# A two-layer transformer block on one core: row sends in turns, owner search over partitions, later roots, idle products in the third kernel

## What is computed

```
xn = layernorm(x)
x  = x + attention0(xn) + ffn0(xn)      # 16 causal heads of 16, residual and norm inside; 2 of 8 experts per sequence
xn = layernorm(x)
x  = x + attention1(xn) + moe1(xn)
```

```
for _ in range(6):                      # iterative inverse of kernel 2, per head 64 x 64
    KV = K @ V
    V = 0.25 * V @ (13*I - KV @ (15*I - KV @ (7*I - KV)))
SV = (kernel1 @ V) @ (kernel3 @ v);  out = SV @ w_proj
```

## Time and profile before

| what | us |
|---|---|
| median of three runs | 2002.76 |
| the profiled execution | 2008.18 |
| its span in the trace | 2006.5 |
| TensorE busy | 1745.2 (87%) |
| VectorE busy | 1530.2 (76%) |
| ScalarE busy | 1015.0 (51%) |
| GpSimd busy | 538.1 (27%) |
| granted TensorE clock, mean | 0.951 |

### The profile page before, as it was taken

One profiled execution on the slowest core, in us unless ns is written; L12 is line 12 of the kernel. 1 busy time (PEld: TensorE's weight loads), 2 busy tenths in 40 slices (PEclk: granted clock), 3 DMA queues, 4 the chain that ended last, 5 costly groups with the idle time before them and its releaser, 6 DMA issues. The chain is left out here.

```text
span 2006.5 us, 34424 instructions
## 1 busy us (share of the span) xinstructions
PE 1745.2 (87%) x11935; PEld 926.1 (46%) x12021; DVE 1530.2 (76%) x3643; ACT 1015.0 (51%) x1941; POOL 538.1 (27%) x623
## 2 busy tenths in 40 slices
PE   0898946889999999999999978978677888999998
PEld 0465621223232323232323235645575657888854
DVE  7997649988988989898999938678566994444456
ACT  3464422566767676767676835357413544232210
POOL 0343243000000000000151010045405884666610
PEclk9999976999999999999999988998787999999999
DMA  3466575005040505050551155122215224666566
GB/s 105 152 199 220 186 193 117 1 2 162 2 163 2 162 3 162 3 148 17 153 139 52 43 183 173 64 80 90 95 46 203 97 94 124 192 186 191 166 227 218
DMA packets 162940, 241.33 MB, mean 120 GB/s; under 512 B 21939, under 2 KB 131507, under 8 KB 161107
## 3 DMA queue, kind: packets, MB, share of 16 engines
q1 hardware_dynamic: 126930, 155.08, 25.9%
q0 software_dynamic: 23136, 75.65, 10.7%
q10 hardware_dynamic: 12704, 8.39, 1.4%
HBM read 118.86 MB, written 119.82 MB: 119 GB/s over the span
## 5 line engine op out<-in xcount | busy, mean ns | idle before, releaser
L1118 ACT ACTIVATE c_prob<-c_pst 128x512 f32<-128x512 f32 (+1 forms) x1152 | 578.8, 578 | 301.5 <-PE c_pst L1083 122.9
L1226 DVE TENSOR_REDUCE c_mx<-c_pf 128x2 f32<-128x1024 f32 x384 | 459.4, 1221 | 35.2 <-PE c_pf L1060 31.9
L1079 PE MATMUL c_pst<-c_qa,c_ka 128*128 128x512 bf16 (+3 forms) x1194 | 339.2, 355 | 14.4 <-DMA c_qa<-c_mT 5.8
L1095 PE MATMUL c_po<-c_prob,c_vh 128*32 128x512 f32 (+3 forms) x2560 | 295.7, 544 | 1.0 <-ACT c_prob L1118 0.4
L1060 PE MATMUL c_pf<-c_ka,c_qa 64*128 64x512 bf16 (+3 forms) x1280 | 230.1, 367 | 50.3 <-DMA c_ka<-s_kbias 22.5
L1222 DVE CUSTOM_DVE_ANT_0 c_spare<-c_pf,c_cut 128x384 f32<-128x384 f32 (+3 forms) x512 | 230.8, 491 | 28.6 <-PE c_pf L1060 24.3
L1079 PEld LDWEIGHTS c_pst<-c_qa,c_ka 128*128 128x128 bf16 x1280 | 110.2, 97 | 202.8 <-ACT c_prob L1118 110.1
L1060 PEld LDWEIGHTS c_pf<-c_ka,c_qa 64*128 64x128 bf16 x1280 | 59.4, 93 | 311.7 <-DVE c_mx L1226 122.2
L992 POOL IOTA c_zero<- 128x24 int32 x6 | 1.3, 214 | 632.3 <-PE c_po L1095 632.3
L2218 POOL DMA_INDIRECT s_parts<-x_yr,x_tags x144 | 140.4, 975 | 85.5 <-DVE x_yr L2867 62.8
L2852 DVE TENSOR_TENSOR x_h<-x_ps,x_sg 128x256 f32<-128x256 f32 x72 | 30.6, 425 | 142.0 <-ACT x_sg L2821 142.0
(11 more groups left out here) (440 smaller groups left out, 3027.1 us busy)
## 6 DMA issues: line engine op xcount, KB each, us to landing
s_slots<-c_zero POOLq DMA_DIRECT2D x6, 3264.0 KB, 17.0
x_xr<-s_slots SPq DMA_DIRECT2D x72, 272.0 KB, 2.8
x_rows<-s_parts SPq DMA_DIRECT2D x8, 2048.0 KB, 8.9
c_qa<-s_qs SPq DMA_DIRECT2D x64, 192.0 KB, 7.3
c_ka<-s_ks SPq DMA_DIRECT2D x64, 192.0 KB, 7.5
s_qs<-b_parts SPq DMA_DIRECT2D x32, 256.0 KB, 2.4
s_ks<-b_parts SPq DMA_DIRECT2D x32, 256.0 KB, 2.7
s_vs<-b_va SPq DMA_DIRECT2D x32, 256.0 KB, 3.8
```

The lines of the kernel that those rows point to most:

```text
L1079: mm = nc.tensor.matmul(pst[:, u % NS, at:at + qn], ka[:, s, hh, kt * P:(kt + 1) * P], qa[:, s, hh, qb * QB + q0:qb * QB + q0 + qn], start ...
L1095: mm = nc.tensor.matmul(po[HV * h:HV * h + HV, q0:q0 + qn], vh[:, s, kt, h, :], prob[:, a % NP, h, at:at + qn], start=(kt == 0), stop=(a i ...
L1118: nc.scalar.activation(prob[:, g % NP, hh, 0:w], pst[:, u % NS, 0:w], ACT.Exp).then_inc(exp_ok, 1)
L1226: nc.vector.tensor_reduce(mx[:, fh:fh + 2, qt, part], pf[:, slot, :, 0:kn], AX.X, ALU.max).then_inc(max_ok, 1)
```

## The change

It changes six of the seven blocks:

- `attention`: the rows of the last head group go out by SP, in four DMAs, each when its part is ready.
- `join_and_project`: `wr` is no longer loaded but copied from `w` by GpSimd, in four instructions; `root(0)` of chunk m moves one step later on ACT, behind `take_queries`; `attended` moves to the front of VectorE's step.
- `landmarks_and_kernel3`: the scatters lose their pacing, alternate between two buffers, and have a semaphore for each buffer; TensorE waits for `o_ok` and runs six idle bf16 products at the end of each step from pair 3 on.
- `inverse`: the owner search lies on 128 partitions x 2 tiles instead of 1 x 144, is split over four iterations, stands ahead of the complement instead of behind it, and comes back to one partition through DRAM.
- `kernel1`: identity and head mask are those of the third kernel; SP issues a residual tile first and one expert load after it in each step; TensorE starts on a part of `kbd`.
- `experts`: the identity isn't made again.

The core of the diff:

```diff
@@ attention, sync
+            for a in range(NB):
+                sp.wait_ge(att_ok, (NQ - 1) * NB + a + 1)
+                sp.dma_start(att_dram[:, NQ - 1, a * 4:a * 4 + 4, :], att[:, (NQ - 1) % 2, a * 4:a * 4 + 4, :]).then_inc(last_out, 16)
             sp.wait_ge(x1_out, 16 * NCH)
+            sp.wait_ge(last_out, 16 * NB)
@@ attention, gpsimd
-                pool.wait_ge(att_ok, n * NB + NB)
-                pool.dma_start(att_dram[:, n:n + 1], att[:, n % 2:n % 2 + 1]).then_inc(att_out[n % 2], 16)
+                if n < NQ - 1:
+                    pool.wait_ge(att_ok, n * NB + NB)
+                    pool.dma_start(att_dram[:, n:n + 1], att[:, n % 2:n % 2 + 1]).then_inc(att_out[n % 2], 16)
@@ join_and_project, sync
-            for k in range(K):
-                for h in range(2):
-                    sp.dma_start(turned(wr[:, k, :])[:, :, h], turned(wqkv[k * P:(k + 1) * P, 0:2 * C])[:, :, 1 - h]).then_inc(wr_in, 16)
@@ join_and_project, gpsimd
+                if n == 0:
+                    halves = lambda a: a.rearrange("p (i h c) -> p i h c", h=2, c=P // 2)
+                    pool.wait_ge(wp_in, 16)
+                    for k in range(K):
+                        for h in range(2):
+                            nc.gpsimd.tensor_copy(halves(wr[:, k, :])[:, :, h], halves(w[:, k, 0:2 * C])[:, :, 1 - h]).then_inc(wr_ok, 1)
@@ join_and_project, scalar and vector
-            in_turn([(2, NCH, root(1)), ..., (1, N, take_queries), (1, NCH, normalise(0, o, o, normed)), (0, NCH, root(0)),
+            in_turn([(2, NCH, root(1)), ..., (1, N, take_queries), (1, NCH, root(0)), (1, NCH, normalise(0, o, o, normed)),
-            in_turn([(2, NCH, second_norm), (1, NCH, normed_attention), (0, NCH, attended), ...
+            in_turn([(0, NCH, attended), (2, NCH, second_norm), (1, NCH, normed_attention), ...
@@ landmarks_and_kernel3, gpsimd
-                wait(pool, sent, 16 * done)
+                wait(pool, sent[g % 2], 16 * (g // 2 * TOPK + k) * RG)
...
+            for pair in range(NR // RG // 2):
+                for k in range(TOPK):
+                    for g in (2 * pair, 2 * pair + 1):
                         tag(g, k)
+                        send(g, k)
@@ landmarks_and_kernel3, tensor
                 turn_half(n, 1, r)
+                if n >= 3:
+                    wait(pe, o_ok, n - 1)
+                    idle_products(6)
@@ inverse, vector
+                if it == 0:
+                    weigh_places(TOPK - 1)
+                elif it == 1:
+                    weigh_shares(TOPK - 1)
+                elif it == 2:
+                    compare_owners(TOPK - 1)
+                elif it == 3:
+                    find_owners()
                 if it < LAST:
                     complement(it + 1)
-                if it == 0:
-                    find_place_and_share(TOPK - 1)
-                elif it == 1:
-                    compare_owners()
-                elif it == 2:
-                    find_owners()
@@ inverse, sync
+            sp.wait_ge(owners_ok, 1)
+            sp.dma_start(owner_dram.rearrange("(p j) -> p j", p=P), owner_i[:]).then_inc(owners_out, 16)
+            sp.wait_ge(owners_out, 16)
+            sp.dma_start(owner[:], owner_dram[0:NT].unsqueeze(0)).then_inc(owners_out, 16)
+            sp.wait_ge(owners_out, 32)
@@ kernel1
-            load_ahead(sp)
-            staggered(sp, N, DEPTH, [(6, load)])
+            def weights(n, u, s):
+                if n < WEIGHTS:
+                    load_weights(sp, n)
+            staggered(sp, N, 0, [(0, load), (0, weights)])
-            set_identity(nc, pool, ident, id0, id_ok)
-            step(nc.gpsimd.memset(hm[:], 1.0))
...
-            dve.wait_ge(hm_ok, 1)
             for bk in range(B * K):
-                ins = nc.vector.tensor_tensor(kbd[:, bk], ...)
-            ins.then_inc(kbd_ok, 1)
+                nc.vector.tensor_tensor(kbd[:, bk], ...).then_inc(kbd_ok, 1)
```

More of the change, by code:

```diff
@@ L1863, in landmarks_and_kernel3 @@
     send_in = [sem(f"r_send_in{i}") for i in range(2)]
-    sent, place_ok = sem("r_sent"), sem("r_place_ok")
+    sent = [sem(f"r_sent{i}") for i in range(2)]
+    place_ok = sem("r_place_ok")
     BM = QL.shape[1]
     H8 = P // D
-    hm = sb("l_hm", [P, H8])
     ones2 = sb("l_ones2", [P, P])
@@ L1921, in tag @@
             def tag(g, k):
-                done = (g * TOPK + k) * RG
-                wait(pool, sent, 16 * done)
+                wait(pool, sent[g % 2], 16 * (g // 2 * TOPK + k) * RG)
                 wait(pool, place_ok, k)
@@ L1930, in tag, with send @@
                     pool.wait_ge(send_in[g % 2], 16 * (g // 2 + 1))
-            def send(g, k, half):
-                for i in range(half * RG // 2, (half + 1) * RG // 2):
-                    scatter(nc, slots_dram, place[:, k, g * RG + i:g * RG + i + 1], send_rows[:, g % 2, i, :]).then_inc(sent, 16)
-            for n in range(NPR):
-                g, k = divmod(n, TOPK)
-                for half in range(2):
-                    wait(pool, ex_ok, 2 * n + half)
-                    if half == 0:
+            def send(g, k):
+                for i in range(RG):
+                    scatter(nc, slots_dram, place[:, k, g * RG + i:g * RG + i + 1], send_rows[:, g % 2, i, :]).then_inc(sent[g % 2], 16)
+            for pair in range(NR // RG // 2):
+                for k in range(TOPK):
+                    for g in (2 * pair, 2 * pair + 1):
                         tag(g, k)
-                    send(g, k, half)
-            pool.wait_ge(sent, 16 * NR * TOPK)
+                        send(g, k)
+            for i in range(2):
+                pool.wait_ge(sent[i], 16 * NR // 2 * TOPK)
         @block.tensor
@@ L2219, in scatter, with inverse @@
                                         in_offset=None)
-def inverse(nc, KTb, Vb, VTb, tbd, W, comb, route_of, place, share, owner, rows_dram, xrows, TOPK, NPR, ITERS, ctx):
+def inverse(nc, KTb, Vb, VTb, tbd, W, comb, route_of, place, share, owner, rows_dram, owner_dram, xrows, TOPK, NPR, ITERS, ctx):
     sb = lambda name, shape, dt=F32: ctx.enter_context(nc.sbuf_tensor(name, shape, dt))
@@ L2385, in find_owners @@
                 both(ts, ownerf[:], ownerf[:], float(E - 1), None, ALU.min)
-                both(nc.vector.tensor_copy, owner[:], ownerf[:])
                 lanes.join(0)
+                nc.vector.tensor_copy(owner_i[:], ownerf[:]).then_inc(owners_ok, 1)
             def polynomial(s, dst, e, scale):
@@ L2617, in expert_weights, with load, experts @@
     w_in = nc.alloc_semaphore(name="x_w_in")
-    def load(eng):
-        for e0, n, gs, us, ds in ((0, E, gw, uw, dw), (E, NSH, sgw, suw, sdw)):
-            for k in range(C // P):
-                eng.dma_start(gu[:, k, e0:e0 + n, 0:I], gs[k * P:(k + 1) * P]).then_inc(w_in, 16)
-                eng.dma_start(gu[:, k, e0:e0 + n, I:2 * I], us[k * P:(k + 1) * P]).then_inc(w_in, 16)
+    def load(eng, piece):
+        shared, kind = divmod(piece, 2 * (C // P) + 1)
+        e0, n, gs, us, ds = (E, NSH, sgw, suw, sdw) if shared else (0, E, gw, uw, dw)
+        k, up = divmod(kind, 2)
+        if kind == 2 * (C // P):
             eng.dma_start(d[:, e0:e0 + n, :], ds).then_inc(w_in, 16)
+        else:
+            eng.dma_start(gu[:, k, e0:e0 + n, up * I:(up + 1) * I], (us if up else gs)[k * P:(k + 1) * P]).then_inc(w_in, 16)
     return gu, d, w_in, load
-def experts(nc, turned_dram, gu, d, w_in, owner, y4_space, x2, slots_dram, parts_dram, out_dram, N, C, I, E, NSH,
+def experts(nc, turned_dram, gu, d, w_in, ident, owner, y4_space, x2, slots_dram, parts_dram, out_dram, N, C, I, E, NSH,
             TOPK, ctx):
@@ L2984, in two_layers @@
                                 landmarks_and_kernel3(nc, QL, KL, QLr, KS, *stacked, qbd, KT, V1[:].rearrange("p b q t e -> p (b q) t e"), tbd, unused, comb, route_of, consts, place, share,
-                                                      rows_dram, slots, TOP_K, T, M, DA, NPR, c)
+                                                      rows_dram, slots, TOP_K, T, M, DA, NPR, hm, ident, c)
                         with ExitStack() as c:
-                            inverse(nc, *stacked, tbd, W, comb, route_of, place, share, owner, rows_dram, xrows, TOP_K, NPR, ITERS, c)
+                            inverse(nc, *stacked, tbd, W, comb, route_of, place, share, owner, rows_dram, owner_dram, xrows, TOP_K, NPR, ITERS, c)
                     gu, d, w_in, load = expert_weights(nc, gate_w, up_w, down_w, sh_gate_w, sh_up_w, sh_down_w, C, I, E, NSH, lm)
                     with ExitStack() as c:
-                        kernel1(nc, QT, KS, W, w_proj, x1, load, place, share, xrows, slots, B, T, C, M, DA, c)
+                        kernel1(nc, QT, KS, W, w_proj, x1, load, hm, ident, place, share, xrows, slots, B, T, C, M, DA, c)
                     with ExitStack() as c:
-                        experts(nc, turned, gu, d, w_in, owner, xrows, QT, slots, parts, flat(out), N, C, I, E, NSH, TOP_K, c)
```

(1 more changed line is left out.)

77 lines of the change are left out of this document (35 added, 42 removed).

## The result

The changed kernel takes 1975.17 us (median of four runs, 1969.35 to 1976.15), the kernel before, on the same chip, 2003.92 (four runs, 2001.23 to 2006.53). The ratio is 0.9851, with an interval from 0.9827 to 0.9875: 29 us less, and not the 39 I forecast; it lies above my range. The profiled execution took 1975.8 us (before: 2008.18).

A forecast was written before the change was run, and what follows sets the result against it. No engine was taken to bound the whole, as blocks follow each other. Terms of -4.0, +2.0, -9.5, -1.5, -19.7 and -6.4 sum to -39.1 us: 2002.76 becomes 1963.7, stated as 1963.5, range 1955 to 1972.

The forecast's parts named there:

- Attention's end: End of attention: with SP issuing the last store, the next part starts at 1173.3 instead of 1177.3; -4.0 us.
- The join: Join: earlier arrival of chunk 1 restarts TensorE sooner (-1.4), but the later root lengthens the loop (+3.4); together +2.0 us.
- the sum of the loop: Join, three steps after TensorE's restart: 14.8 us root to root instead of 13.0, summed as 46.0 against 42.65; +3.4 us.
- Kernel 3's end: End of kernel 3: unpaced scatters finish near 1412, so the block ends with VectorE at 1438.0, not 1447.5; -9.5 us.
- Rival (a): Block ends: the 7 us belong to the end of GpSimd's list in any block; 8 us less won, 1971.5; chance 0.08.
- Rival (c): Kernel 3: dense scatters take memory access from VectorE, making the kernel slower than before; chance 0.02.
- Idle products: Kernel 3 steps: TensorE's idle products gain one of three half-clock stretches; -1.5 us, bounds -6 and +2.6.
- rival (b): Kernel 3: the idle products hold the clock up throughout; 4.5 us more won, 1959; chance 0.10.
- Inverse: Inverse: the owner search on 128 partitions shortens the periods between complements to 7.3 us; sum -19.7 us.
- 4.1 in iteration 1: Start of the inverse: 4.1 us saved in iteration 1, whose polynomial then waits for 2.4 us of place search.
- Kernel 1: Kernel 1: GpSimd's scatters start at once (-1.3) and its stop for a residual tile goes (-5.1); together -6.4 us.
- Rival (d): Kernel 1: the stop moves instead of going, a residual tile being late behind the 2 MB load; 1968.5; chance 0.10.

The follow-up runs named there:

- e8: The changed kernel, but attention's last rows, in the same four parts, are issued by GpSimd and not by SP; 1980.41 us, launched once.
- e7: The changed kernel with kernel 3's scatters paced by the exponentials again, in the new order and with two semaphores; 1971.16 us, launched once.
- e13: The kernel before with kernel 3's scatters no longer paced, their order and single semaphore kept; 2003.69 us, launched once.
- e14: The kernel before with the inverse's rows in sixteen loads of 256 KB; 2002.40 us, launched once.
- e1: The changed kernel with the inverse's two 2 MB loads cut into sixteen of 256 KB, each held back for one more VectorE stage; 1972.97 us.
- e11: The changed kernel, but in kernel 1 SP issues all ten expert weight loads ahead of the residual tiles; 1977.46 us, launched once.
- e5: The changed kernel with the old orders of ACT and VectorE in the join and the inverse's rows in sixteen loads; 1968.67 us.
- e4: The changed kernel without kernel 3's six idle products per step and their wait; 1974.87 us.

## Why the prediction was off

*Attention's end*: right. -4.0 forecast for the gap, 7.9 to 3.3 measured, and e8 shows the reason. The block's last write scatters from 1163.7 to 1170.3 over these profiles, with either code, which a forecast made on one profile can't contain; the one before, at 1169.5, was a late one.

*The join*: the arrival was right (1197.5 forecast, 20.2 us into the block; 20.3 measured, mostly 21 to 21.6), and so was the restart (-1.4 forecast, -1.5 measured). The step that failed is the sum of the loop, "Over the three steps ... that is 46.0: +3.4". Its mechanism and its price per step were right: 14.8 in place of 13.0, 1.8 more, where 1.3 to 1.6 more were measured. But three steps at 1.8 are +5.4, or 48.1, and not 46.0; 47.7 were measured. Half the clock behind the stop is not the reason: it lasts 10.2 us there before and after, and the way from the restart to chunk 2 grew by only 0.5. Over the profiles the join is 5.1 longer, not 2.0. The rest of the difference is an arrival that mostly came later than in the profile after, so that the restart is only 0.6 earlier in the mean, and in four of the eight profiles another 3.4 us at half the clock, 83 us into the block, which cost them 1.7 us each. The 256-byte pieces: the loads' removal brought chunk 1 forward by 1.3 to 2.6 us, 5.4 in one profile. The higher price of short pieces (the Trainium skill, DMA: Bandwidth & Descriptors, Specifications), by which I estimated that the arrival would move by 4, is not what these rows show, that one profile apart.

*Kernel 3's end*: right in size (-9.5 forecast; the block went from 10.2 us behind its last division to 0.5), wrong in the part that it gave to the pacing. I wrote that without pacing the scatters end early; the two semaphores do that by themselves (e7), and taking the pacing away alone leaves half (e13). Rival (a), that 7 us stand at every end of GpSimd's list, is refuted by the 0.3 us between the end of the last division and the inverse. Rival (c), VectorE losing its memory access, too: VectorE was busy 78.3 us between the divisions beside unpaced scatters, 79.0 before. The rule of a port that VectorE and GpSimd lock for each other (the Trainium skill, SBUF — State Buffer, SBUF: two separate sides) shows no effect in these rows: the median of the scatters is 974 ns, 971 before, and the longest 1461 ns, 1182 before.

*Idle products*: -1.5 forecast, -2.4 to -3.3 measured, since they keep up the clock in more of the stretches than the one I counted: rival (b) in mechanism, at half its price. What they bring was lost again in some profiles at the start of kernel 3, where the first division came 32.7 to 35.8 us into the block. It follows the time at 0.50 ahead of it: up to 6.8 us of it in the profiles with 32.7 and 32.8, 10.2 to 13.7 in those with 34.1 to 34.9, and 17.1, most of it in the windows shown above, in the profile after. That differed between profiles of the same code, before and after, and has no cause shown here.

*Inverse*: the term that was mis-sized most. From iteration 2's first complement on it went as worked out (7.27 a period, 15.5 saved against 15.1). But the start, for which I counted 4.6 saved (4.1 and 0.5), took 20.7 us, as before (20.1). The step that failed: "4.1 in iteration 1, whose polynomial now waits for 2.4 us of place search". I had not asked what was late next. TensorE's stops of 0.49 and 2.54 us with no releaser stand in the trace of before too, beside the two loads, and the second was partly hidden by the search. With the search gone they came bare, and with them half the clock. Where the loads are spread the start takes 14.3 to 15.1 us, and 17.8 on the kernel before (e14). So, one after the other, the loads cost 2.4 us of the start before, the search 2.8, and the loads 5.7 in the profile after: with spread loads the start is 5.2 shorter than before (e1), and the 4.6 of the forecast would have come.

*Kernel 1*: -6.4 forecast, -6.2 measured, but its parts were -1.3 and -5.1 in my sum and are 0 and -6.4 in e11. Rival (d) did not occur.

*Experts*: I gave them nothing. They take 332.5 to 332.7 in all four profiles on the kernel before, and 334.2 to 334.9 in ten of the thirteen others. Behind TensorE's stop at the shared experts (2.2 us after, 1.8 before) the clock is at 0.66 for 5 us in the profile after, and at 1.00 before. Eight of the ten show this fall, and neither the three fast ones nor the four on the kernel before do. The two left (e1, e5) have 6.8 us at half the clock at the block's start and not 3.4, but e4, e13 and e14 have that too, at 332.5 to 332.7. Why the fall comes more often after the change is open.

## What to carry to other kernels

Before a stop is credited as gained, look for the second one that it hides: rows with the releaser "issue" beside full DMA engines will be there when the cover is gone. Large loads that nobody needs soon are worth cutting and pacing, since they also stopped an engine that waited for no data: 53.0 us of inverse became 49.3 to 50.6. A price per step counts once for every step: three times 1.8 is 5.4, and not 3.4. Two moves in a software pipeline have to be tried in all combinations, and a block's length from one profile is not a measurement: an arrival that came 4 us early made the worst inference of this study.

## What the hardware showed

A block went on 6.2 to 7.2 us after the end of the issue of its last DMA where GpSimd issued it (before, e8, e13), and 3 us after where SP did (after). With the DMA engines at 350 GB/s, TensorE stood still for 0.5 to 3.5 us at a time in the middle of products that wait for nothing new, in all thirteen profiles with the two 2 MB loads; in the four with sixteen of 256 KB no such stop was above 0.7 us. Every one of these stops ended 1.4 to 1.6 us after a 16 KB packet of an instruction queue. And the same code in kernel 3 found its clock at 0.50 from 5.4 us on in the profile after and at 1.00 until at least 10 us in the sixteen others, with the same idle times of 1.07 and 0.83 us ahead of it.
